# A two-layer transformer in one kernel: a reordered first stretch, and a rotation whose halves are exchanged by on-chip transfers

## What is computed

```
xn = layernorm(x);  x = x + attention0(xn) + W2 gelu(W1 xn + b1) + b2
xn = layernorm(x);  x = x + attention1(xn) + W3 (silu(W1' xn + b1') * (W2' xn + b2')) + b3
```

```
rot = concatenate([-x2, x1]);  rope(x) = x * cos + rot * sin
```

## Time and profile before

| | us |
|---|---|
| median of three runs | 615.9 |
| lowest and highest | 614.74, 620.51 |
| the profiled execution | 613.84 |
| span of its instructions | 612.1 |

### The profile page before, as it was taken

The page is one execution under the profiler, slowest core; times in us unless marked ns, Lnnn a source line. Parts: engine busy times, 40 slices in busy tenths (PEclk is TensorE's granted clock), DMA queues, the critical chain, the costliest instruction groups (busy, mean ns, idle before and its releaser), DMA issues.

```text
span 612.1 us, 10518 instructions
## 1 busy us (share of the span) xinstructions
PE 563.1 (92%) x3216; PEld 441.4 (72%) x3216; DVE 458.6 (75%) x1232; ACT 347.9 (57%) x598; POOL 234.4 (38%) x346
## 2 busy tenths in 40 slices
PE   4789799999999999989999999989889989997997
PEld 3687568777777877767777687767677767775755
DVE  6477967755575777567789588898989788788764
ACT  4556476756465672666664676447644664556451
POOL 7313324543303522212223114354744285554332
PEclk9988999999999999999999999999999999999999
DMA  6884541353233244315434314335442346343101
GB/s 197 145 238 144 139 121 64 109 156 97 77 87 101 74 120 139 87 58 150 111 115 138 88 40 133 87 87 135 126 112 79 78 135 164 111 122 104 36 3 69
DMA packets 30535, 67.02 MB, mean 109 GB/s; under 512 B 4880, under 2 KB 18192, under 8 KB 28560
## 3 DMA queue, kind: packets, MB, share of 16 engines
q1 hardware_dynamic: 21840, 38.04, 23.0%
q0 software_dynamic: 8640, 28.32, 15.8%
HBM read 50.87 MB, written 13.63 MB: 105 GB/s over the span
## 4 chain that ended last, share of the span: by engine, by line
PE 73%; DVE 10%; issue 5%; DMA 4%; ACT 4%; POOL 2%; SPq 0%; ACTq 0%; DVEq 0%; POOLq 0%
PE banks L745 47%; PE banks L805 8%; PE banks L852 8%; PE banks L830 8%; DMA q_sb<-max_t 2%; DVE banks L1137 2%; DMA q_sb<-stage 1%; DMA raw<-in_attn 1%; DVE x_res L1181 1%; ACT L987 1%; DVE neg_max L1137 1%; PE banks L833 1%; POOL raw L634 1%; PE banks L765 1%; DVE neg_max L1142 1%
## 5 line engine op out<-in xcount | busy, mean ns | idle before, releaser
L968 ACT ACTIVATE probs<-banks 128x512 f32<-128x512 f32 (+1 forms) x256 | 137.1, 546 | 178.3 <-PE banks L830 141.3
L745 PE MATMUL banks<-xnT,w_up 128*128 128x512 f32 x576 | 150.4, 398 | 3.0 <-DVE v_sb L1117 1.3
L1142 DVE TENSOR_REDUCE neg_max<-banks 128x2 f32<-128x512 f32 x128 | 87.6, 688 | 85.4 <-PE banks L805 85.0
L745 PE MATMUL banks<-w_down,hid 128*128 128x512 f32 x480 | 127.4, 400 | 6.2 <-ACT hid_f L988 4.0
L745 PEld LDWEIGHTS banks<-xnT,w_up 128*128 128x128 f32 x576 | 103.2, 190 | 21.8 <-DVE x_res L1181 1.6
L805 PEld LDWEIGHTS banks<-k_sb,q_sb 96*128 96x128 f32 x512 | 93.3, 193 | 29.9 <-issue 5.6
L805 PE MATMUL banks<-k_sb,q_sb 96*128 96x256 f32 (+1 forms) x512 | 101.0, 279 | 11.5 <-DMA q_sb<-stage 3.5
L1137 DVE CUSTOM_DVE_ANT_0 banks<-banks,mask_qk 128x128 f32<-128x128 f32 (+1 forms) x256 | 86.0, 374 | 29.7 <-PE banks L805 29.6
L745 PEld LDWEIGHTS banks<-w_down,hid 128*128 128x128 f32 x480 | 85.2, 188 | 24.3 <-ACT hid_f L988 5.5
L687 POOL TENSOR_SCALAR_AFFINE_SELECT probs<-probs 128x256 f32<-128x256 f32 x128 | 59.8, 467 | 83.8 <-ACT probs L968 76.3
L745 PE MATMUL banks<-xnT,w_qkv 128*128 128x256 f32 x576 | 85.1, 296 | 3.7 <-DVE hid_f L1191 1.8
(11 more groups left out here) (80 smaller groups left out, 662.5 us busy)
## 6 DMA issues: line engine op xcount, KB each, us to landing
q_sb<-q_parts SPq DMA_DIRECT2D x60, 256.0 KB, 4.5
raw<-in_up POOLq DMA_DIRECT2D x48, 256.0 KB, 3.3
raw<-in_down POOLq DMA_DIRECT2D x40, 256.0 KB, 3.0
q_parts<-stage SPq DMA_DIRECT2D x30, 256.0 KB, 2.8
raw<-in_attn POOLq DMA_DIRECT2D x20, 256.0 KB, 3.7
k_parts<-stage SPq DMA_DIRECT2D x14, 256.0 KB, 2.5
k_sb<-k_parts SPq DMA_DIRECT2D x14, 256.0 KB, 4.1
out<-x_res SPq DMA_DIRECT2D x8, 256.0 KB, 2.2
```

The costliest lines, as they stand in the source:

```text
L745: mm = nc.tensor.matmul(out_ap, lhs(a), rhs(b_), start=first and j == 0, stop=stop and j == 2, **kw)
L968: nc.scalar.activation(probs[:, k % PROBS, 0:w], banks[:, ST_BANKS[k % 2], 0:w], ACT.Exp, scale=SCALES[n // B]).then_inc(exp_done, 1)
L1142: nc.vector.tensor_reduce(maxima[:, 2 * g:2 * g + 2, t], banks[:, bank_of[x], :].rearrange("p (r t) -> p r t", r=2)[:, :, 0:w], AX.X, ALU. ...
```

## The change

There are two groups of edits. In the front: the fills of the query buffers go behind the first `up` product and between the first maxima; the second `up` product is brought forward, ahead of the first maxima; the row of maxima is sent ahead of the next key store, and the output biases are loaded after it, into `rot_a` instead of into a buffer for probabilities; POOL holds the loads of weight pieces 8 to 11 until the first queries have landed in place (`first_q`); and the statistics and Newton steps of the layer norms are cut into pieces over several slots, those of batch 3 in unit 1 instead of unit 0. In the rotation: SP copies each half of `qkv_v` to the other half of `rot_b` by two transfers inside SBUF (`swap`, due in slot 1), DVE multiplies all 128 partitions by sines at once and adds (`turn`, now slot 3), and `round` and `store` move to slot 5.

```diff
@@ followers
     if x[0] == "qkv":
-        return [(1, ("drain", x)), (2, ("turn", x)), (4, ("round", x)), (4, ("store",) + x[1:])]
+        return [(1, ("drain", x)), (2, ("swap", x)), (4, ("turn", x)), (6, ("round", x)), (6, ("store",) + x[1:])]
...
+        if c == 1:
+            return [(0, ("hidden", 0, 0)), (0, ("hidden", 0, 1)), (10, ("hidden_lo", 0, 0)), (11, ("hidden_lo", 0, 1))]
@@ start_slots
-    o += [[("xn", 0, 0), ("xn", 0, 1)] + split(0, "attn", 0, 1) + [("fill", 0), ("fill", 1)]]
+    o += [[("xn", 0, 0), ("xn", 0, 1)] + split(0, "attn", 0, 1)]
...
-    o += [[("xn", 1, 0), ("xn", 1, 1), ("fill", 2)] + split(0, "up", 0, 1)]
+    o += [[("xn", 1, 0), ("xn", 1, 1)] + split(0, "up", 0, 1)]
...
-    o += [parts(("up", 0, 0, 0)) + [("load_q", 2), ("load_bias",)]]
+    o += [parts(("up", 0, 0, 0)) + [("load_q", 2), ("fill", 0)], parts(("up", 0, 1, 0))]
...
-    later = parts(("up", 0, 1, 0)) + parts(("qkv", 1, 0)) + [("bias",)]
+    later = parts(("qkv", 1, 0))
...
-    ms[8] += [("mt", 0), ("mrow", 0)]
+    ms[1].append(("fill", 1))
+    ms[4].append(("fill", 2))
+    ms[7].append(("mrow", 0))
+    ms[8] += [("mt", 0), ("load_bias",)]
@@ unit_slots
-        slots[3] += [("stats", 0, 2), ("stats", 0, 3)]
-        slots[6] += [("rstd", 0, 2), ("rstd", 0, 3)]
+        slots[5].append(("bias",))
+        slots[2].append(("stats", 0, 2, 0))
+        slots[3].append(("stats", 0, 2, 1))
+        for j in range(3):
+            slots[4 + j].append(("newton", 0, 2, j))
...
@@ sync engine
+                if x[0] == "swap":
...
+                    sp_.wait_ge(wk_copied, cp[x] + 1)
+                    if hips[x]:
+                        sp_.wait_ge(staged_lo, hips[x])
+                    sp_.dma_start(rot_b[0:64, 0:w, :], qkv_v[64:P, 0:w, :]).then_inc(swapped, 16)
+                    sp_.dma_start(rot_b[64:P, 0:w, :], qkv_v[0:64, 0:w, :]).then_inc(swapped, 16)
@@ gpsimd
-                    if EARLY <= k + RAW < len(pieces):
+                    if k == EARLY + 1:
+
+                        pool.wait_ge(first_q[0], 64)
+                        for j in range(RAW):
+                            load(EARLY + 2 + j)
+                    elif EARLY + 2 <= k and k + RAW < len(pieces) or k in (EARLY - RAW, EARLY - RAW + 1):
                         load(k + RAW)
@@ scalar engine
-                    if k == PROBS - 1:
-                        act.wait_ge(bias_summed, 1)
@@ vector engine
-                    nc.vector.tensor_tensor(rot_b[0:64, 0:w, :], qkv_v[64:P, 0:w, :],
-                                            other[64:P].to_broadcast([64, w, T]), ALU.mult).then_inc(rot_sin, 1)
-                    nc.vector.tensor_tensor(rot_b[64:P, 0:w, :], qkv_v[0:64, 0:w, :],
-                                            other[0:64].to_broadcast([64, w, T]), ALU.mult).then_inc(rot_sin, 1)
                 if x[0] == "turn":
...
+                    dve.wait_ge(swapped, 32 * (hips[x] + 1))
+                    nc.vector.tensor_tensor(rot_b[:, 0:w, :], rot_b[:, 0:w, :],
+                                            table[:, 1:2, :].to_broadcast([P, w, T]), ALU.mult).then_inc(rot_sin, 1)
```

More of the change, by code:

```diff
@@ L110, in with_followers @@
 def with_followers(slots):
-    due = [[] for _ in range(len(slots) + 5)]
+    due = [[] for _ in range(len(slots) + 7)]
     o = []
@@ L187, in unit_slots @@
     if u == 0:
-        slots[3] += [("stats", 0, 2), ("stats", 0, 3)]
-        slots[6] += [("rstd", 0, 2), ("rstd", 0, 3)]
+        slots[5].append(("bias",))
[3 more added lines that the diff above has]
+            slots[4 + j].append(("newton", 0, 2, j))
+    if u == 1:
+        slots[2].append(("stats", 0, 3, 0))
+        slots[3].append(("stats", 0, 3, 1))
+        for j in range(3):
+            slots[4 + j].append(("newton", 0, 3, j))
     if s == 0 and B <= n + 2 < 2 * B:
         c = n + 2 - B
-        slots[3].append(("stats", 1, c))
-        slots[7].append(("rstd", 1, c))
+        slots[2].append(("stats", 1, c, 0))
+        slots[4].append(("stats", 1, c, 1))
+        for j in range(3):
+            slots[5 + j].append(("newton", 1, c, j))
     if s == 3 and n + 2 < 2 * B:
@@ L434, in build @@
         first_q = [sem(f"first_q{j}") for j in range(2)]
+        swapped = sem("swapped")
         st_filled = sem("st_filled")
@@ L1026, in _ @@
                 if x[0] == "stats":
-                    _, L, b = x
+                    L = x[1]
                     tiles = stat_tiles(x)
-                    for t in tiles:
+                    for t in tiles[x[3]:x[3] + 1] if x[3:] else tiles:
                         if L == 0:
@@ L1037, in _ @@
                     link(ins)
+                    if x[3:] and x[3] == 0:
+                        continue
                     t = slice(tiles[0], tiles[-1] + 1)
@@ L1043, in _ @@
                         link(ins)
[L1044 removed]
+                if x[0] == "newton":
                     tiles = stat_tiles(x)
                     t = slice(tiles[0], tiles[-1] + 1)
[L1048 to L1055 removed]
+                    if x[3] == 0:
+                        link(nc.vector.tensor_scalar(dev[:, t].bitcast(I32), var_e[:, t].bitcast(I32), 1, None, ALU.arith_shift_right))
+                        link(nc.vector.tensor_scalar(rstd[:, t].bitcast(I32), dev[:, t].bitcast(I32), -1, GUESS, ALU.mult, ALU.add))
+                    link(nc.vector.tensor_tensor(rs0[:, t], rstd[:, t], rstd[:, t], ALU.mult))
+                    link(nc.vector.scalar_tensor_tensor(out=rs1[:, t], in0=rs0[:, t], scalar=-0.5, in1=var_e[:, t],
+                                                        op0=ALU.mult, op1=ALU.mult))
+                    link(nc.vector.scalar_tensor_tensor(out=rstd[:, t], in0=rs1[:, t], scalar=1.5, in1=rstd[:, t],
+                                                        op0=ALU.add, op1=ALU.mult))
                 elif x[0] == "rstd":
@@ L1242, in _layouts @@
     row = np.arange(P) // 8
-    rope = np.stack([cos[row % 8], np.where((row < 8)[:, None], sin[row % 8], -sin[row % 8])], 1).astype(np.float32)
+    rope = np.stack([cos[row % 8], np.where((row < 8)[:, None], -sin[row % 8], sin[row % 8])], 1).astype(np.float32)
     c = np.ascontiguousarray
```

25 lines of the change are left out of this document (5 added, 20 removed).

## The result

The changed kernel takes 636.75 us in the median of four runs (632.69 to 641.79), the kernel before 615.39 us beside it (614.74 to 620.51): a ratio of 1.033, with an interval of 1.024 to 1.043. The forecast was 610.2 us with 601 to 620, so it was wrong, and on the side to which rival (b) had been given 0.11. The profiled execution spans 631.0 us.

The account below looks back on a forecast made before the run. PE, busy 563.1 of 612.1 us, was taken as the bound, so only its idle time or low clock could give time. 613.84 - 8.6 (front) + 5.0 (rotation) = 610.2 us, range 601 to 620.

Parts of the forecast that it names:

- rival (b): In twelve units the row of maxima queues behind the store's bytes on SP and lands late: 633 us, chance 0.11.
- The front, -8.6: Start of the kernel to unit 1: PE's waits and a slow-clock stretch shrink, -1.26 - 3.47 - 1.7 - 0.7 - 1.5 = -8.6 us.
- the 1.26: PE's wait before the first `up` product goes, with 1.90 us of fills no longer ahead of it: -1.26 us.
- the 3.47: PE's wait for queries before the first maxima goes, as queries land before PE arrives: -3.47 us.
- both slow stretches: Front, PE at low clock: 32 to 40 us expected to go, -1.7 us; 40 to 50 us (1.7) left as is.
- the row's 1.68: PE's wait before unit 0 for its row of maxima: 0.7 us of it taken as gain, bounds 0 and -3.4.
- unit 1's 3.14 for DVE: PE's wait in unit 1 behind DVE's Newton steps: half expected to go, -1.5 us, bounds 0 and -3.1.
- The rotation, +5.0: Layer 1: later rounding and store delay units 17, 19, 23, 16 and 20, unit 21 gains: 1.4 + 0.5 + 2.3 + 1.7 - 0.9 = +5.0 us.
- two issues 0.98, landing 1.9: Units 17, 19, 23: after the low part, SP's issues take 0.98 us, then the row of maxima lands in 1.9.
- the 0.85 foretold for unit 20: Key units 16 and 20: DVE's product and addition move into the backlog PE waits for, +0.85 us each.
- The transfers, costed at nothing: The swap's two transfers per query pair land in 3 us, before DVE needs them some 4 us later: no cost.
- DVE's saving: One product replaces two in the rotation: 1.2 us less DVE work per query pair, credited as -0.9 in unit 21.

Follow-up runs that it names:

- unused transfers behind the loads: Front-only kernel plus each rotated pair's two transfers, read by nobody, issued on SP behind the key and query loads: 609.86 us, ratio 0.988.
- store from POOL: Changed kernel with the rotated pair's store issued by POOL behind its own rounding, SP not waiting for the low part: 624.11 us, ratio 1.006.
- store from POOL and SP waiting: Changed kernel with POOL issuing the rotated pair's store, SP still waiting for the low part at the store's old place: 625.36 us, ratio 1.013.

## Why the prediction was wrong

**The front, -8.6: right, in part by luck.** -8.0 at unit 2 in the profile, and 10.3 and 7.0 us between the medians of the two series. The terms miss in both directions: the 1.26 went; the first maxima came at 29.5 as worked out, but by the moved product alone, not by the held loads, and 1.25 of the 3.47 stayed; both slow stretches went, not one; of the row's 1.68, 0.78 was left, near the 1.0 assumed, though in other executions of this front it is 4.2, a loss of 2.5 where the bounds were gains of 0 to 3.4; unit 1's 3.14 for DVE went, replaced by two waits for ACT's steps, 2.32 and 1.38 us, so that the -1.5 did not come there. And layer 0 did give something back, 1.3 us in units 8 to 11.

**The rotation, +5.0: the step that failed.** Measured +25.6. The step is the last of "two issues 0.98, landing 1.9". The places were right: units 17, 19 and 23, and the store directly ahead of the row. Their price was not: 1.4 + 0.5 + 2.3 = 4.2 foretold, 10.0 measured. From the end of the low part to the row's landing the prediction has 0.98 + 1.9 = 2.9 us; it took 5.1, 4.4 and 4.5, because the rows landed after 4.0, 3.4 and 3.5 us. That is 5.2 of the 5.8 us missing. I had taken the median of all rows for rows that go out right behind 512 KB and, what I did not look at, beside a weight load from POOL. Rival (b) had the place, and the point from which I let it decide, about 2 us of added landing, is what unit 17 shows (4.0 - 1.9); its cause, the store's bytes alone, is not enough, since directly behind a store without a weight load the row landed after 2.1 us, in unit 23 of the kernel before too, where I could have read it. The Trainium skill, page "DMA: Bandwidth & Descriptors", section "Queues, rings and completion order", has an engine's descriptors consumed in ring order; the row does land after the store that is ahead of it, but that order doesn't set the price by itself: 2.1 us behind the store alone, 3.4 to 4.0 with a weight load from POOL's queue beside it.

Of the 20.6 us between +5.0 and +25.6, these three units are 5.8 and the units behind them, at the low clock, 7.5 (8.3 less the 0.85 foretold for unit 20). Units 25 and 27 are 3.4, which I had left out as having room; units 12 to 16 are 2.6 more than the 0.85 foretold for unit 16; and unit 21, with a loss of 0.2 for the gain of 0.9, is 1.1.

**The clock, not in the sum at all.** I had read from the earlier trace rows that stretches at 1.2 GHz follow a wait, and used it as a gain in the front; the same reading should have priced every wait that the rotation makes longer. It is 8.3 us, against the 10.0 of the three units with the waits. That rival (b)'s 633 lies near the measured 636.75 is luck: it priced landings in twelve units, and no clock.

**The transfers, costed at nothing: nearly right here, with a wrong landing.** They landed later than the 3 us taken (4.3 in the median), and DVE still waited only once, because in this kernel it comes late to the product; that once is unit 27, with 2.5 us. The unused transfers behind the loads put the bytes at 3 us at most, by the profiles. But nothing in my text saw that SP waits at the swap for ACT, with the query loads behind it, which costs 9 us as soon as the swap stands one slot earlier.

**DVE's saving.** 0.88 us per pair of queries, not 1.2. In unit 15, POOL's and DVE's timeline:

```profile
370.48 1.30 POOL L732 TENSOR_TENSOR x_res<-x_res,bias_out 128x512 f32<-128x512 f32 x1
371.95 1.54 POOL L732 TENSOR_TENSOR x_res<-x_res,bias_out 128x512 f32<-128x512 f32 x1 [0.17 <-POOL x_res L732]
```

```profile
370.85 1.50 DVE L1125 TENSOR_TENSOR rot_b<-rot_b,table 128x512 f32<-128x512 f32 x1
372.37 1.67 DVE L1129 TENSOR_TENSOR rot_b<-rot_b,rot_a 128x512 f32<-128x512 f32 x1
```

Alone these take 0.69 us. The Trainium skill, page "SBUF — State Buffer", section "Who interferes with whom", says that a DVE instruction with two SBUF inputs contends with a GpSimd instruction that reads SBUF. The trace agrees in unit 15 and for the product of unit 23 (1.31 us), and I had set the rule aside because the old additions showed no stretching; of those only one had met an addition of POOL, for 0.4 us, and moved by two slots three pairs do. In units 17 and 21, whose credits I had put in doubt by this rule, the product took 0.69 and 0.68 us. What was saved moved no time anyway: DVE was not what PE waited for in the units that decide, and the credit of 0.9 in unit 21 was a loss of 0.2.

**Open.** How the long landings divide between store and weight load, as no experiment moved the load. What the store from POOL still loses without SP's wait, since its profile isn't used; with SP's wait, stops of 2.59 and 2.66 us remain ahead of units 18 and 24. What units 12, 15 and 16 lose, 0.9 to 1.0 us each, which no experiment took apart (0.85 was foretold for unit 16). And theory C was never tried by itself, a product in slot 3 with everything else as before.

## What to carry to other kernels

When a step is put off by some slots, look on each in-order queue at what then stands right behind it, and also at who needs its result: here the store slid in front of an 8 KB row for which TensorE waits, moved behind that row it was late for the loads that read it, and one slot earlier it costs 18 us less. Price a small urgent transfer by rows of the trace with the same neighbours, those on other engines' queues included, not by the median of all; and where TensorE stops for several us add what its clock loses afterwards, here 8.3 us on top of 10.0. And try the parts of a change apart: this one held a gain of 7 to 10 us and a loss of 26.

## What the runs showed of the hardware

- An 8 KB row landed 1.8 to 1.9 us after its issue on a quiet queue, 2.1 us with a store of 512 KB issued right ahead of it (units 15 and 27), 3.4 to 4.0 us where POOL had issued a weight load of 256 KB 0.2 to 0.4 us before as well (units 17, 19, 23), 2.7 to 2.8 us where such a load left 0.1 to 0.8 us behind the row (units 21, 25), and 6.3 to 6.4 us amid the front's traffic.
- Transfers of 64 and 128 KB inside SBUF landed after 2.3 to 6.8 us, and two per pair more, read by nobody and issued behind the loads, cost nothing between the medians (609.9 against 610.1 us) and 2 to 3 us in the profiles.
- After stops of 5.2 to 5.7 us TensorE's granted clock was 0.54 to 0.76 over the next 7 us, behind the stop of 0.78 us ahead of unit 0 it was 1.00. The units behind the three long stops took 2.5 to 3 us longer than before. With the store from POOL and SP waiting, stops of 2.59 and 2.66 us were followed by 0.72 (416 to 422 us) and 0.55 (507 to 514 us).
- Two-input products and sums on DVE over 128x512 took 0.69 us alone and 1.31 to 1.67 us where POOL's addition of the same kind was already under way; one that POOL's met 0.4 us after its start took 0.77 (unit 19).
